# Issuing gathers without waiting for the previous ones to land, in a graph attention and expert network kernel

## What is computed

```python
ft = (feat @ W).reshape(n, H, OUT)              # feat: layer norm of x, 12500 x 256; 4 heads of 64
e = e_src[src] + e_dst[dst]                     # one score per edge and head
e = jnp.where(e >= 0, e, 0.2 * e)
ex = jnp.exp(e - emax[dst])
denom = jax.ops.segment_sum(ex, dst, num_segments=n)
a = ex / denom[dst] * dist
out = jax.ops.segment_sum(ft[src] * a, dst, num_segments=n)
x = x + out
x = x + ffn(layernorm(x))                       # router and six experts, two per node
```

## Time and profile before

| | us |
|---|---|
| median of 3 runs | 3480.75 |
| lowest and highest of them | 3477.3, 3482.05 |
| time of the profiled execution | 3484.34 |
| its span in the trace | 3482.6 |

### The profile page before, as it was taken

One profiled execution on the slowest core, in us unless ns is written; L12 is line 12 of the kernel. 1 busy time (PEld: TensorE's weight loads), 2 busy tenths in 40 slices (PEclk: granted clock), 3 DMA queues, 4 the chain that ended last, 5 costly groups with the idle time before them and its releaser, 6 DMA issues. The chain is left out here.

```text
span 3482.6 us, 53251 instructions
## 1 busy us (share of the span) xinstructions
PE 2272.1 (65%) x10832; PEld 1804.6 (52%) x10833; DVE 2034.7 (58%) x4705; ACT 1499.2 (43%) x2731; POOL 2143.6 (62%) x2064
## 2 busy tenths in 40 slices
PE   1672554555555555557667666666664999899995
PEld 1552443444444444445445555455553787777774
DVE  4544444555556667667777878888887833233322
ACT  0661222323333334444455555555553554444442
POOL 0006666666666666666676676666640677777775
PEclk9895777777777777777887888888776999999998
DMA  3444444444444444444454554544445044545453
GB/s 110 144 137 110 117 116 113 123 117 123 123 123 127 124 130 128 132 126 137 128 140 131 137 139 134 136 136 132 127 108 91 20 80 78 80 78 80 78 80 47
DMA packets 231864, 393.51 MB, mean 113 GB/s; under 512 B 55846, under 2 KB 148810, under 8 KB 230897
## 3 DMA queue, kind: packets, MB, share of 16 engines
q0 software_dynamic: 114816, 262.31, 32.9%
q1 hardware_dynamic: 77036, 91.35, 9.5%
q10 hardware_dynamic: 39924, 38.86, 3.4%
HBM read 324.55 MB, written 69.21 MB: 113 GB/s over the span
## 5 line engine op out<-in xcount | busy, mean ns | idle before, releaser
L975 POOL DMA_INDIRECT m_rows<-table,src_col x1568 | 1555.2, 992 | 998.6 <-issue 699.2
L1346 PE MATMUL m_A<-m_msg,m_by_edge 128*128 128x260 f32 x3920 | 1243.3, 483 | 394.2 <-issue 253.4
L1346 PEld LDWEIGHTS m_A<-m_msg,m_by_edge 128*128 128x128 f32 x3920 | 941.7, 247 | 610.2 <-issue 397.2
L1205 ACT ACTIVATE m_apart<-m_drow,nid 128x1024 bf16 x297 | 340.9, 1148 | 958.6 <-SPq L946 930.9
L1052 DVE TENSOR_TENSOR m_msg<-m_rows,m_A 128x2048 f32<-128x2048 f32 (+1 forms) x294 | 568.1, 1932 | 71.4 <-issue 55.7
L1332 PE MATMUL m_E<-m_look_parts,m_by_node 128*128 x2368 | 107.7, 176 | 492.0 <-ACT m_by_node L1208 491.6
L1009 DVE SCALAR_TENSOR_TENSOR m_by_edge<-dst_col,m_less_base,row 128x512 f32<-128x512 f32 x590 | 416.5, 748 | 0.0
L1551 POOL DMA_INDIRECT out<-x_con,x_to_i x206 | 329.1, 1598 | 109.0 <-issue 77.8
L1332 PEld LDWEIGHTS m_E<-m_look_parts,m_by_node 128*128 128x128 bf16 x2368 | 95.6, 99 | 575.4 <-issue 550.8
L1018 DVE TENSOR_REDUCE m_e_sum<-m_E 128x64 f32<-128x192 f32 x295 | 104.9, 356 | 463.4 <-PE m_E L1332 399.6
L1208 ACT ACTIVATE m_by_node<-m_apart,m_one 128x1024 bf16<-128x1024 bf16 x297 | 340.9, 1148 | 9.8
(11 more groups left out here) (246 smaller groups left out, 2341.4 us busy)
## 6 DMA issues: line engine op xcount, KB each, us to landing
m_drow<-dst_row SPq DMA_DIRECT2D x196, 256.0 KB, 3.6
m_rows<-table,src_col POOLq DMA_INDIRECT x1568
ydram<-m_y ACTq DMA_DIRECT2D x49, 264.0 KB
table<-f_rowbuf SPq DMA_DIRECT2D x14, 910.0 KB, 5.2
m_xb<-in_x ACTq DMA_DIRECT2D x48, 256.0 KB
out<-m_x ACTq DMA_DIRECT2D x48, 256.0 KB
f_xin<-in_x SPq DMA_DIRECT2D x13, 896.0 KB, 6.8
x_w<-in_L_ffn_expert_w SPq DMA_DIRECT2D x18, 256.0 KB, 6.0
```

Of the source, the lines that this page charges most:

```text
L975: nc.gpsimd.indirect_dma_start(rows[:, g % RING, j, :], None, table, bass.IndirectOffsetOnAxis(ap=K.src_col[:, g, j:j + 1], axis=0)).then_ ...
L1205: a.activation(apart[i][:, :], drow[:, bass.ds(g % RING, 1), :].rearrange("p a n -> p (a n)"), ACT.Abs, bias=K.nid[:, bass.ds(b, 1)], scal ...
L1346: m = t.matmul(psA[i][:, 0:ROW], by_edge[i][:, j, :], msg[i][:, j, :], start=(j == tiles[0]), stop=(j == tiles[-1]))
```

## The change

The wait of every second group for the landing of the two groups ahead of it is taken out. In its place every group from the fifth on waits for the gathers that filled the same slot four groups earlier. The wait for `slot_free` stays. Nothing else in the kernel changes.

```diff
             for g in range(NG):
                 if g >= RING:
                     pool.wait_ge(slot_free, g - RING + 1)
-                if g and g % 2 == 0:
-                    for r in (g - 2, g - 1):
-                        pool.wait_ge(gathered[r % RING], 16 * GT * (r // RING + 1))
+                if g >= RING:
+                    pool.wait_ge(gathered[g % RING], 16 * GT * (g // RING))
                 gather(g)
```

## The result

| | before | after |
|---|---|---|
| median of four runs, us | 3481.1 | 3307.54 |
| lowest and highest, us | 3477.3, 3482.05 | 3303.63, 3309.84 |
| span of the profiled execution, us | 3482.6 | 3305.4 |

The ratio is 0.9503, with an interval of 0.9489 to 0.9516. The forecast was 3326, between 3285 and 3395. Direction, mechanism and range held; the gain is 173.6 us where 155 was forecast.

What follows compares the result with a forecast made beforehand. Gathers bound the stage's first half, VectorE the end: removing 2.45 us pauses moves the stage end from 2640 to 2475, 165 us, less 10 for the crossing, gain 155. Median 3480.75 becomes 3326, range 3285 to 3395.

Steps and rivals of the forecast that it cites:

- Who binds: Gather stage: gathers bound its first half, VectorE with its chain the end; the change works on the first alone.
- no change: Rival at GpSimd's pauses: the slot is what is waited for, so slot_free still holds GpSimd; 3481 us, chance 0.05.
- The price of a pause: Ahead of every second group's gathers: a pause of 2.76 us removed leaves a 0.305 step, giving 2.45 us.
- A cost that was put at nothing: Gathers beside VectorE's L1009: no lengthening taken; if all took 1.010, 24 us more until 1500.
- The crossing: Where VectorE becomes the bound: latest at t = 1500, 128 saved, share 0.813, end 2475; 10 us off for unsharpness.
- the fourth line of the forecast's list: Starting point t = 1900: 69 pauses, 169 saved; 601.5 us of VectorE work at 0.813 is 740; end at 2471.
- The signs named: Gather stage: no 2.6 us gaps, groups near 10.4 us apart, VectorE above 75% in 1300 to 1500, items ending near 2485.
- Less: Rival in the gather stage: VectorE binds sooner and gathers lengthen; gain 99, 3382 us; chance of less gain 0.16.
- More: Rival in the gather stage: VectorE's idle time shrinks further, nearly all saved by 2200 counts; 195, 3286 us; chance 0.08.
- Slower: the gathers stretch when the queue is never drained: Rival at GpSimd's gathers: undrained, each takes 1.32 us, a group 13.0; 224 us later, 3705 us; chance 0.09.

Runs made afterwards that it cites:

- e1b: Changed kernel with the old landing pause ahead of every second group after group 134 (30 pauses), none before; faster chip: 3310.66 us, ratio 0.9519.
- e2b: Changed kernel with the old landing pause ahead of every second group up to group 134 (67 pauses), none after; faster chip: 3475.18 us, ratio 0.9993.
- e4: Changed kernel with a landing pause ahead of every fourth group only (48 pauses); faster chip: 3387.84 us, ratio 0.9730.
- e3b: Changed kernel with a landing pause ahead of every group (195) in place of the added wait; faster chip: 3669.56 us, ratio 1.0548.
- e5: Changed kernel without the added wait for the gathers of four groups earlier, so no pause; slower chip: 4003.3 us, ratio 1.0221.
- e3: Changed kernel with a landing pause ahead of every group (195 instead of 97); slower chip: 3719.93 us, ratio 0.9485.
- e2: Changed kernel with the old landing pause ahead of every second group up to group 134, none after; slower chip: 3934.45 us, ratio 1.0042.

## Why the prediction was right, and where its sum was off

**Who binds.** Right. The chain from gather over ScalarE and TensorE to VectorE is shorter by what was taken out, and the trace's naming of L963 at the pauses of the earlier trace rows was, as argued, the landing seen through SyncE: with the `slot_free` wait still in place those waits are gone. The rival "no change" fell with that, and `e1b` against `e2b` shows it a second time.

**The price of a pause.** Right: 2.45 us. `e4` agrees at half the number, to 5 us in 83; at twice the number `e3b` has 2.32. By group 105, 52 pauses have gone, 127 us.

**A term that the sum did not have.** The forecast said that pauses are the only idle time of the gathers beyond 0.30. They are not. In the trace of before, behind the first gather after a pause, there is at some groups a second gap:

```profile
433.47 0.95 POOL L975 DMA_INDIRECT m_rows<-table,src_col  x1 [2.61 <-SPq L963]
436.31 0.96 POOL L975 DMA_INDIRECT m_rows<-table,src_col  x1 [1.88 <-issue]
```

It stands in groups 14, 26, 38 and so on to 182, every twelfth, 15 times, always 1.87 or 1.88 us, which is 1.57 above the ordinary step. It needs the pause ahead of it. `e2b` has it in groups 14 to 134 and in none after (2.18 us once); `e1b` has it in 146 to 182 and in none before (1.47 us the first time). `e4`, whose pauses never stand ahead of group 14 or one that is twelve further, has none, and the changed kernel none either: at these places no step of theirs is over 0.45 us. By group 105 that is 8 of them, 12.6 us; by 139 it is 11, 17.3 us. The rows that show it were in the list of idle time by "issue", which the forecast took to hold ordinary steps only. A count of the steps of that list by their length would have found it.

**A cost that was put at nothing.** The forecast took no lengthening of the gathers and allowed for 24 us at the most. Summed gather by gather, they take 7.0 us more up to group 105 and 9.3 more up to 139, and the first one starts 0.6 later. Of the 840 gathers up to group 105, 199 overlap an L1009 of VectorE (L1008 in the profile after) by more than 0.1 us before and 240 after; these take 1.07 us in the mean in both traces, the others 0.96. The reason for taking no growth, that VectorE does the same L1009s per group, missed that more of them can fall on a gather. The Trainium skill's rule on the shared interface (GPSIMD Engine Reference, Specifications), that GpSimd and VectorE contend when a VectorE instruction has two SBUF inputs, agrees with the 1.07 against 0.96. That a busier VectorE as such slows the gathers is not borne out: in `e3b` VectorE is busy 51% of the time up to group 105, where it was 56% before, and the gathers still take 7.9 us more, 224 of them beside an L1009. The sum at group 105 is then 127 + 13 - 8 = 132, measured 131.3. At group 139 it is 69 pauses, 169 + 17 - 10 = 176, measured 175.7. Without the second gaps the lengthening would have shown. Together the two missing terms are worth some 5 to 7 us; that they nearly hide each other is luck.

**The crossing.** This is where most of the difference lies. The forecast's sum found the latest starting point at t = 1500, with 128 us saved, VectorE at 0.813 from there and 10 us off because a crossing is not sharp. In the trace that work (group 105 and on, 896.6 us of VectorE's busy time by the earlier trace rows) is reached at 1500 - 131 = 1369 and finished at 2465.8: a share of 0.8175. Its busy share is 0.829 between 1500 and 1700 and 0.825 in the next 200 us; no stretch of the earlier trace rows shows more than 0.813, though a single 100 us of the trace before, 2100 to 2200, does with 0.824. At 0.8175 instead of 0.813 the same work ends 6 us sooner. Saved 131 instead of 128 is 3 more. The 10 us were not lost: the measured gain at the end, 173.0, is within 3 us of the 175.7 that GpSimd had saved when it first ran out of slots, and four slots are enough to pass the crossing. Then 155 + 3 + 6 + 10 = 174, and the stage ends 173.0 earlier. This sum is bound to close, since 0.8175 is worked out from the measured end: VectorE's own busy time between 1369 and 2465.8 is 893.5 us, a share of 0.815, so that some of the 6 us is work that lies elsewhere. How the 16 us divide between the share and the crossing is not shown. What is measured without it: from the start of group 139 to the end of the last item it is 745.0 us before and 747.6 after. With slots first waited for at 1718, the crossing is not at 1500 of before but at 1894 (group 139), which was the fourth line of the forecast's list.

**The signs named.** The 2.6 us gaps are gone. Groups are 10.3 us apart at the start, 10.5 around group 100, as the 10.4 said. VectorE is at 78% between 1300 and 1500 (over 75% was named). Waits for L963 begin at 1718, later than the "some 1500". Items end at 2465.8 rather than 2485, for the reasons above. ScalarE's wait for L946 is 657.7 in all, where 808 stood for 273 to 1700 alone. The experts' stretch is the same but for 4 us.

**The rivals.** "Less" fell: the gathers' growth was a third of its bound and VectorE's share above its own. "More" stated that nearly all saved until 2200 counts, 195 us; 183 was saved at most, at group 152, and 10 of these were given back in slot waits. "Slower: the gathers stretch when the queue is never drained" is wrong for the run of the forecast: the median gather is 0.955 us with 1568 issued and no landing waited for, and the sum of the gathers grew by 0.7%. The overfull descriptor buffer of which the Trainium skill speaks (Perfetto Trace Analysis, DMA Instruction — SWDGE (GPSIMD)) shows as such in no run here; before the first slot wait every step of the changed kernel is 0.31 us or less. A slower kernel nevertheless came about on the slower chip, and there too the gathers do not stretch.

## What to carry to other kernels

Where the issuing engine is what everyone waits for, a wait for its own transfers ahead of further issue costs time on each pass, here 2.45 us, and the wait for the free slot is enough to keep the order. The gain of such a change lasts until the next engine is late, so the sum has to be made from the point of the crossing, with the busy share that the engine reaches when it is truly the bound; a long stretch of the trace before may lie below it. Measure such a change on more than one chip before it is kept: taking these pauses out was worth 5% on the faster chips and, without the added wait, cost 2% on the slower one.

## What the runs showed that was not expected

**Sequencers that slow down on one chip.** On the chip where before takes 3917 us, the gathers themselves are the same: 951, 957 and 1704 ns at least, in the median and at most in the kernel with no pause (e5). Its waits for slots are seven times those of the changed kernel on a faster chip. In its trace:

```profile
L975 POOL DMA_INDIRECT m_rows<-table,src_col x1568: 951/957/1704, 272.3 to 3108.4; - x196
...
  SPq L963: 828.1, 115
  issue: 678.1, 1453
```

The engines' own instruction queues show what is slow. SyncE's slot release is a single semaphore instruction. Its least, median and greatest duration in ns, first in that trace, then in the changed kernel's trace on a faster chip:

```profile
L963 SPq EVENT_SEMAPHORE  x192: 15/17/702, 310.1 to 3098.5; - x192
```

```profile
L963 SPq EVENT_SEMAPHORE  x192: 17/17/17, 308.4 to 2413.4; - x192
```

Only 4 of these 192 are slow in `e5`, but other instructions of the queues are too. Loads of registers, DMA issues and drains are left out of what follows, since some of them take 0.55 to 1.2 us in the trace of before too (62, 267 and 6 in the queues of SyncE, VectorE and ScalarE). In stretches of the trace most of the others take some 0.70 us: between 301 and 333, 16 of 19 in SyncE's queue and 16 of 19 in VectorE's, though none of 16 in ScalarE's. Counting the others of 0.55 to 1.2 us in the three queues over the whole trace gives 123, 399 and 192 in `e5`; 118, 377 and 207 with late pauses alone; 117, 377 and 183 with early pauses alone; and 5, 153 and 55 with a pause for every group. The traces of the faster chips, before and after among them, have 0 in all three. Most of the stretches begin 5 to 29 us into a run of gathers without a pause, and end no later than 3 us after GpSimd stops. Of the 714 slow instructions in `e5`, 709 lie between 4 us after the start of such a run and 3 us after its end, which is two thirds of that time. VectorE in order of time, in the first of them in `e5`:

```profile
323.53 0.75 DVE L1006 SCALAR_TENSOR_TENSOR m_by_edge<-dst_col,m_less_base,row 128x512 f32<-128x512 f32 x1 [1.66 <-issue]
326.44 0.75 DVE L1006 SCALAR_TENSOR_TENSOR m_by_edge<-dst_col,m_less_base,row 128x512 f32<-128x512 f32 x1 [2.16 <-issue]
340.55 0.36 DVE L1015 TENSOR_REDUCE m_e_sum<-m_E 128x64 f32<-128x192 f32 x1 [13.35 <-remote]
341.18 0.19 DVE L1022 TENSOR_TENSOR m_z<-m_e_sum,m_rows 128x32 f32<-128x32 f32 x1 [0.28 <-DVE m_e_sum L1015]
```

The instructions keep their length, 0.75 us for L1006, but 1.7 to 2.2 us pass between them with nothing to wait for. From 341 on the steps are short again; GpSimd stands then for want of a slot, 10.35 us until 344.67. I read this as a loop: slow sequencers make the items late, late items hold the slots, GpSimd stops, and the sequencers recover. A pause for every group leaves fewer and shorter stretches and is the fastest of the four there. The order of the four times is that of the counts: 714, 702, 677 and 213 for 4003, 3993, 3934 and 3720 us. No run tests the loop itself. The granted clock of TensorE does not tell the chips apart: it is 0.805 in both traces with a pause for every group, `e3` and `e3b`.

Between 400 and 1500, where on a faster chip VectorE waits mainly for look-ups and GpSimd for no slot, this kernel shows ("remote" where the trace names no engine):

```profile
DVE m_e_sum L1015 <- remote: 410.0, 44, 21.9
...
POOL m_rows L975 <- SPq L963: 277.0, 39, 16.2
```

What makes the sequencers slow is open. It goes with long runs of gathers without a drain, on this chip and not on the faster ones. No trace of the kernel before was taken on that chip, so that its own 3917 us can't be put down to the same stretches; and the kernels with half or none of the gathers, which could tell whether the gathers are needed for it, ran on a faster chip alone.

**The second gap of 1.88 us** in every twelfth group after a pause, shown above, was not expected either. Its cause is open. It comes behind the same gathers in all kernels that have a pause there, each 96 behind the last, and not in those that pass these places without one. It also depends on how long GpSimd had stood: behind an idle time of 4.5 us or more ahead of such a group, the second step is 0.44 or 0.45 us in every trace (group 194 before: 7.60, then 0.45), and in `e2` on the slower chip six of its eleven places have 1.87 us and the other five, behind 4.07 to 7.45 us, have 0.44 or 0.45.
